# Two cross attentions: projections, splitting and stacks two slots sooner, the maxima's transfers ahead of the stacks'

## The reference, cut to what matters

```python
x = x + g_msa * (attn(rope(q), rope(k), v, mask) @ attn_out_W)   # self attention, 128 keys
x = x + g_x * (attn(xc @ cq_W, ctx @ ck_W, ctx @ cv_W) @ co_W)   # first cross attention, 77 keys
x = x + g_mlp * (gelu(xm @ mlp_W1 + b1) @ mlp_W2 + b2)
x = x + (attn(xq @ Wq + bq, xkv @ Wkv + bkv) @ Wp + bp)          # second cross attention, 77 keys
```

## Time and profile before

| | |
|---|---|
| median of three executions | 1186.53 us (1183.35 to 1187.0) |
| the profiled execution | 1197.59 us, span 1195.8 us |
| busy share of the span | PE 90%, ACT 71%, POOL 72%, DVE 69%, PEld 52% |
| granted TensorE clock, mean | 0.946 of full |
| self attention's units | from 81.2 us (L812 of unit 0) |
| first cross attention's units | 428.5 to 718 us |
| second cross attention's units | from 908.9 us |

### The profile page before, as it was taken

How to read it: one execution, slowest core, us unless ns; L and a number is a source line. 1 busy time by engine, 2 the same in 40 slices (tenths; PEclk the granted TensorE clock), 3 DMA queues, 4 the chain that set the end, 5 groups by cost and what they waited for, 6 DMA issues and landing times.

```text
span 1195.8 us, 42336 instructions
## 1 busy us (share of the span) xinstructions
PE 1080.7 (90%) x16226; PEld 616.5 (52%) x16226; DVE 825.0 (69%) x2195; ACT 851.5 (71%) x1527; POOL 856.6 (72%) x1804
## 2 busy tenths in 40 slices
PE   5779999999998889888998888999998999999987
PEld 4435555555544445554554553444444566666665
DVE  4358888888887878777887662322325888878775
ACT  2347776777766688787887667787875878878765
POOL 2578888888886678677887424676887878888742
PEclk9789999999998999898999679999998999999988
DMA  6766567665664566666766610000315677777761
GB/s 164 182 129 109 103 111 136 107 108 101 110 111 78 77 102 94 100 102 100 106 99 105 97 20 1 1 0 1 57 20 73 113 119 124 124 119 127 117 111 33
DMA packets 165018, 110.40 MB, mean 92 GB/s; under 512 B 42553, under 2 KB 164434, under 8 KB 164818
## 3 DMA queue, kind: packets, MB, share of 16 engines
q1 hardware_dynamic: 161744, 105.97, 52.8%
q10 hardware_dynamic: 3074, 1.72, 0.6%
HBM read 9.71 MB, written 4.19 MB: 12 GB/s over the span
## 4 chain that ended last, share of the span: by engine, by line
PE 54%; ACT 11%; POOL 8%; SPq 7%; DMA 6%; DVE 5%; issue 5%; ACTq 1%; POOLq 0%; DVEq 0%
PE ps_po L535 10%; PE ps_pj L433 7%; SPq L1004 6%; PE ps_st L514 6%; DMA stacks<-mt 6%; PE ps_nat L486 5%; ACT p L812 5%; PE ps_pj L416 5%; PE ps_pj L411 4%; PE ps_st L547 4%; PE ps_po L556 4%; PE ps_nat L471 3%; PE ps_pj L424 3%; DVE negmax L619 2%; ACT nrm L781 2%
## 5 line engine op out<-in xcount | busy, mean ns | idle before, releaser
L619 DVE TENSOR_REDUCE negmax<-ps_nat 128x8 f32<-128x616 f32 (+1 forms) x384 | 360.6, 939 | 62.3 <-PE ps_nat L486 51.9
L812 ACT ACTIVATE p<-ps_st 128x1024 f32<-128x1024 f32 (+1 forms) x256 | 261.3, 1021 | 165.2 <-PE ps_st L514 164.2
L535 PE MATMUL ps_po<-p,vz 77*32 77x128 f32 (+1 forms) x6144 | 262.0, 291 | 4.7 <-DVE mt L627 2.2
L514 PE MATMUL ps_st<-stacks 64*77 64x128 bf16 (+1 forms) x3072 | 161.0, 227 | 39.2 <-DMA stacks<-mt 28.9
L812 ACT ACTIVATE p<-ps_st,key_bias 77x1024 f32<-77x1024 f32 x128 | 142.1, 1110 | 62.0 <-PE ps_st L514 60.9
L535 PEld LDWEIGHTS ps_po<-p,vz 77*32 77x32 f32 (+1 forms) x6144 | 153.4, 113 | 46.3 <-issue 13.5
L896 POOL TENSOR_TENSOR ot<-vv,den 128x128 f32<-128x128 f32 x192 | 87.7, 457 | 122.7 <-ACT den L800 111.6
L486 PEld LDWEIGHTS ps_nat<-stacks 64*128 64x128 bf16 x3072 | 79.7, 98 | 138.8 <-issue 125.4
L486 PE MATMUL ps_nat<-stacks 64*128 64x77 bf16 (+1 forms) x3072 | 136.4, 211 | 10.4 <-DVE negmax L619 7.2
L514 PEld LDWEIGHTS ps_st<-stacks 64*77 64x77 bf16 (+1 forms) x3072 | 109.9, 113 | 53.4 <-issue 26.9
L627 DVE COPY mt<-ps_po 128x128 bf16<-128x128 bf16 x192 | 42.5, 221 | 112.5 <-PE ps_po L500 112.2
(11 more groups left out here) (149 smaller groups left out, 2112.0 us busy)
## 6 DMA issues: line engine op xcount, KB each, us to landing
stacks<-parts SPq DMA_DIRECT2D x512, 128.0 KB, 3.3
stacks<-parts SPq DMA_DIRECT2D x256, 77.0 KB, 2.8
stacks<-mt SPq DMA_DIRECT2D x192, 32.0 KB, 2.8
p<-in_x_dram SPq DMA_DIRECT2D x16, 256.0 KB
out_dram<-part SPq DMA_DIRECT2D x16, 256.0 KB, 2.3
ot<-in_ctx_dram SPq DMA_DIRECT2D x8, 154.0 KB
gated<-in_ctx_dram SPq DMA_DIRECT2D x8, 154.0 KB
stacks<-in_L_xcond_adaLN_W_dram SPq DMA_DIRECT2D x1, 576.0 KB, 4.3
```

The source lines that it names most:

```text
L514: m = t.matmul(c.ps_st[h][0:nk, S * g:S * g + S], kst[half(h), par, at, nk * j:nk * j + nk], qst[half(h), par, at, S * j:S * j + S], start ...
L535: m = t.matmul(c.ps_po[step % 2][32 * g:32 * g + 32, S * p:S * p + S], c.vz[0:nk, i % 2, step % G, g, at:at + 32], c.p[0:nk, hh, S * g:S * ...
L619: v.tensor_reduce(c.negmax[:, step % 2, :].rearrange("p (h q g) -> p h q g", h=2, q=2)[:, :, p, :], c.nat_pair[:].rearrange("p (h n) -> p ...
L812: a.activation(c.p[0:nk, 2 * p:2 * p + 2, :].rearrange("p h n -> p (h n)"), c.st_pair[0:nk, :], ACT.Exp, bias=bias).then_inc(exped, 1)
```

## The change

1. `head_of(i)`: in both cross attentions b becomes u - 22. With it q, k, the norm's three jobs (centring 13 slots ahead of b for all groups that are not placed early), the splitting on ACT and POOL and the stack transfers all come two slots sooner. For groups 16 to 19 the norm comes three slots sooner, since it was 12 ahead of b. Group 35's norm moves from slots 289 and 290 to 281 and 282, as early jobs in the MLP.
2. `v` moves from u-2 to u-4 in the cross attentions. `o` moves from u+16 to u+15 for groups 14 to 31, and in the second cross attention `o` from u+16 to u+14 and `o2` from u+17 to u+15. DVE's reading of the first cross attention's o thereby goes from an odd slot to an even one. The last group's o stays.
3. SP: `bring_max` stands ahead of the slot's stack transfers, in all attentions. In the cross attentions the 16 stack transfers are spread over seven slots in place of six, two in each slot that has a maximum: modulo 8, 1 (two), 2 (three), 3 (two), 4 (three), 5 (two), 6 (three), 7 (one).
4. `key_slots` is b+8 instead of b+7: an even slot.

Modulo 8 the first cross attention has afterwards on PE: m 0, q 1, k 3, v 4, c 5, o 7.

```diff
+def head_of(i):
+    return slot_of(PER * i) - LEAD - (2 if i >= NG else 0)
...
-            b = slot_of(PER * i) - LEAD
+            b, u = head_of(i), slot_of(PER * i)
...
-            if 2 * NG <= i < 2 * NG + 4:
-                self.norm_early(("n", i), b - 6)
+            if i < NG:
+                self.norm(("n", i), b - 6, 3 if i >= 1 else 0)
+            elif 2 * NG <= i < 2 * NG + 4:
+                self.norm_early(("n", i), b - (6 if i < 2 * NG + 3 else 12))
             else:
-                self.norm(("n", i), b - (6 if i < NG else 12 if i < NG + 4 else 13), 3 if 1 <= i < NG else 0)
-            self.add(self.late, b + (14 if i < NG else 18), ("v", i))
-            if i < 2 * NG:
-                self.add(self.late, b + LEAD + (17 if i < NG - 2 else 16), ("o", i))
-                self.add(self.late, b + LEAD + (17 if i < NG - 2 else 16), ("o2", i))
-            else:
-                self.add(self.late, b + LEAD + (12 if i == GROUPS - 1 else 16), ("o", i))
-                self.add(self.late, b + LEAD + (12 if i == GROUPS - 1 else 17), ("o2", i))
+                self.norm(("n", i), b - 13)
+            self.add(self.late, u - (6 if i < NG else 4), ("v", i))
+            first, second = (u + 12, u + 12) if i == GROUPS - 1 else (u + 14, u + 15) if i >= 2 * NG else (u + 15, u + 15) if i >= NG - 2 else (u + 17, u + 17)
+            self.add(self.late, first, ("o", i))
+            self.add(self.late, second, ("o2", i))
...
-            key_slots = {slot_of(PER * i) - LEAD + 7: i for i in range(NG, 2 * NG)}
+            key_slots = {head_of(i) + 8: i for i in range(NG, 2 * NG)}
...
-                      1: ((7, 0, (0, 1, 2)), (8, 0, (3,)), (8, 1, (0, 1)), (9, 1, (2, 3)), (9, 0, (4,)), (10, 0, (5, 6, 7)), (11, 1, (4, 5, 6)), (12, 1, (7,)))}
+                      1: ((7, 0, (0, 1)), (8, 0, (2, 3, 4)), (9, 1, (0, 1)), (10, 1, (2, 3)), (10, 0, (5,)), (11, 0, (6, 7)), (12, 1, (4, 5, 6)), (13, 1, (7,)))}
...
+                if even(unit_at(slot + 3)):
+                    bring_max(unit_at(slot + 3) // 2)
                 for i, x, t in at_slot.get(slot, []):
                     bring_stack(i, x, t)
-                if even(unit_at(slot + 3)):
-                    bring_max(unit_at(slot + 3) // 2)
```

More of the change, by code:

```diff
@@ L827, in _ @@
                 for r, x, which in steps[min(i // NG, 1)]:
-                    at_slot.setdefault(slot_of(PER * i) - LEAD + r, []).append((which, i, x))
+                    at_slot.setdefault(head_of(i) + r, []).append((which, i, x))
             a.preload_act_table_set("natural_log_exp_and_others")
@@ L1015, in _ @@
                 for r, x, ts in starts[min(i // NG, 1)]:
-                    at_slot.setdefault(slot_of(PER * i) - LEAD + r, []).extend((i, x, t) for t in ts)
+                    at_slot.setdefault(head_of(i) + r, []).extend((i, x, t) for t in ts)
             def fetch(i):
```

## The result

The changed kernel takes 1150.24 us, the median of four executions (1149.43 to 1151.61); the kernel before, timed beside it, takes 1185.3 (1183.35 to 1187.0, four). The ratio is 0.9677, with an interval of 0.9639 to 0.9715: 35 us faster. The prediction was 1162, with a range of 1147 to 1182. The profiled execution of the changed kernel took 1151.61 us with a span of 1149.8; its mean granted clock is 0.968.

The account below looks back on a forecast made before the run. The prediction took PE's stands for late maxima transfers, and half clock behind them, as what could be won. Terms 15.2 + 5.1 + 2.5 + 2 + 4 + 0 + 0 = 28.8 us, 25 carried to the median: 1186.5 - 25 = 1162 us, range 1147 to 1182.

Parts of the forecast that it names:

- What bounds the kernel: Cross attentions: a group takes 16.6 us when nothing is late; PE's avoidable wait is for the maxima's transfer, 28.9 us.
- SP's queue: Cross attentions: bunching starts maxima's transfers late, PE stands beyond 2.4 us lateness; ordering and spreading make these waits nearly vanish.
- at 16.9 each: Eleven groups in each cross attention were to take 16.9 us each, gaining 15.2 us in the first, 5.1 in the second.
- The cost of one transfer: SP's queue: 0.72 us for one transfer, halfway between 0.64 and 0.80; 20 transfers take 14.4 of a group's 16.6 us.
- From the profiled execution to the median: Whole kernel: 25 of the 28.8 us gained against the profiled 1197.6 us carried over to the median of 1186.5.
- The rule on landing: DMA queues: if landing counts rather than starting, order wins nothing and the time stays at 1186.5 us.
- Group 35's norm: Second cross attention's start: moving this norm into the MLP removes PE's 3.86 us wait for POOL; gain 4 us.
- The self attention's end: Norms of groups 16 to 19: new waits against old ones removed, 0; bounds a gain of 4 and loss of 6 us.
- The hidden edits: Cross attentions: jobs turn by two slots together, only o's reading changes its relation; taken as 0, bounds -3 and +5 us.
- Half of it: Rival: stands go, but the clock still falls or groups take 17.4 us; about 1174 us, chance 0.17.
- no change: Rival: landing or ACT is what counts, time stays within 0.3%, at 1186 us; chance 0.08.
- The banks: Slower rival, first cross attention: q takes o's bank, so a late DVE makes PE wait; 1203 us, chance 0.13 for slower.

Follow-up runs that it names:

- run 8: The kernel before with the maxima's transfers issued by ACT, behind its exponential, instead of SP; nothing else moved: 1158.28 us, ratio 0.9706.
- 5: The changed kernel with the old, bunched list of stack transfer starts, the maxima still first: 1163.4 us, ratio 0.9783.
- run 6: The changed kernel with the maxima behind the slot's stack transfers, the spread starts kept: 1171.02 us, ratio 0.9853.
- run 2: The changed kernel with both SP edits undone (old list of starts, maxima last), the other edits kept: 1203.06 us, ratio 1.013.
- run 7: The kernel before with only group 35's norm moved, to slots 283 and 284 instead of 289 and 290: 1188.27 us, ratio 0.999.
- run 4: The changed kernel with the norms of groups 16 to 19 three slots later, where they stood before: 1153.14 us, ratio 0.9663.
- run 11: The changed kernel with the norms of groups 16 to 19 one slot later: 1157.22 us, ratio 0.973.
- run 10: The changed kernel with only the key row moved back to b+7, an odd slot: 1149.02 us, ratio 0.9666.
- 12: The changed kernel itself, unaltered, timed once more: 1151.45 us, ratio 0.9677.
- run 1: The kernel before with one edit, the maxima's transfer ahead of the slot's stack transfers: 1173.65 us, ratio 0.9854.
- run 3: The changed kernel with o of groups 14 to 31 one slot sooner, so DVE reads it in an odd slot: 1175.05 us, ratio 0.9839.
- run 9: The changed kernel with o of groups 14 to 31 and the key row each one slot sooner: 1158.99 us, ratio 0.9745.

## Why the prediction was right, step by step

**What bounds the kernel: right.** The waits for the maxima were the one thing that could go, and a group without them takes what the earlier trace rows showed for the quick one, or less.

**SP's queue: the mechanism was right, its worth was mis-sized.** The chain of the argument (bunching makes the maxima start late, PE stands, the clock drops to its lower level) held at its first links: run 8 for the start, the waits of runs 5 and 6 for both of the two edits, run 2 for nothing else doing it. The last link, from the stand to half clock, holds for the longer stands and not for each (last section). Mis-sized was the term "at 16.9 each": the groups take 16.3 and 16.4. I had taken 16.6 as the floor because no group of before was quicker, and added 0.3 for groups that would not reach it. The floor was a little lower, and all but one of them reached it in the first attention, all but two in the second. That is 5.8 and 5.5 us too little in the two attentions; in the group behind the first eleven it is 3.5 more, and the rest of that attention with the MLP brings 3.5 that I had not counted at all, though its clock of 0.94 stood open to it. Its first 47 us still run at a clock of 0.85 (0.75 before), without a wait for a transfer; PE's longest stand in them is 1.13 us for POOL's splitting. Why the clock falls there is open.

**The cost of one transfer.** I took 0.72 us, between 0.64 and 0.80. The lateness of 1.63 us in slot 7 lies between what 0.72 gives (0.5) and 0.80 (1.95): from slot 1 to slot 7 of a 16.3 us group 12.2 us pass, and (12.2 + 1.6) / 18 = 0.77 us for a transfer. In the stretch shown above it is less, 18 transfers from 562.72 to 575.62, 0.72 each. The tolerance of 2.4 us held, so the figure cost the changed kernel nothing, but it is why run 6 missed.

**From the profiled execution to the median.** I carried 25 of 28.8 us over, since that execution lay 11 us above the median. The profiled executions differ by 46.0 and the medians by 35: the caution was right and too small, 4 us where 11 was due. So the forecast is 12 us too high by two errors that partly cancel: the terms of the sum are 17 us too small, and the step to the median took off 7 us too little. The measured 1150 lies inside the range, 3 us above its lower end, and that the forecast came this near owes something to this cancelling.

**The rule on landing** that I had set against the change (the Trainium skill, "DMA: Bandwidth & Descriptors", section "Issuing engines are not separate DMA queues") says that the time to start a DMA is usually small relative to the DMA. If that decided here, the time would have stayed at 1186.5. Landing stayed at 2.7 to 2.8 us and the time fell by 35 us; run 8 alone gives 2.9% by moving the issue to another engine (1158.3 us beside 1191.8). Here the measurement decides: each start is short against its landing, but 20 of them at 0.72 to 0.77 us take 14 to 15 of a group's 16.3 us, and so their order counts.

**Group 35's norm** was counted at 4 and gave 3.7 in the profile. Run 7 warns against reading it as a gain by itself.

**The self attention's end** was counted at 0 and came out at +1.5, inside the bound of 6. The wait that I named (POOL for the values of group 14) is there with 3.18 us. The old placing is no better by the total (run 4) and one slot later is worse (run 11). A small cost is likely all the same: the five groups take 116.6 to 118.9 us in the four profiles with these lists (the changed kernel, 5, 10 and 12), 113.4 to 115.1 in the four with the heads and norms of before (1, 7, 8 and the kernel before), and 115.6 in run 4.

**The hidden edits** were taken at 0. For the edits as made that holds; the key row in the other slot changes nothing (run 10). But I wrote that the place of `o` is the one relation that changes, and overlooked the key row, which edit 4 moves by one slot and not by two, into the norm's. And my reason, that DVE is not last in a slot, is refuted by run 3: with `o` one slot sooner the copy of the maxima is late behind a DVE instruction that has tripled, and each group costs 1.2 us more. I had looked at the sums of work per slot and not at what runs beside what.

**The rivals.** Half of it and no change did not come. The banks did not make PE wait: in the changed kernel it waits once for a reading of `o` (L420 for L663), 0.8 us, and that behind the first cross attention's units.

**The signs I had named.** The wait for `mt` is under 5 us, and the 3.86 us wait at the second's start is gone. The groups take 16.2 to 16.3 us, just under the 16.4 to 17.0 named. "Within 1 us of its copy's end" is met in slots 1, 3 and 5 and missed in slot 7, with 1.63 us at the median.

## What to carry to other kernels

Where an engine waits for a transfer, take the time from the producer's end to the start of the issue, and compare it with the lateness at which the first waits appear; a queue that is fast enough on the average can still be late by its own bunching. Putting one transfer first moves the lateness to those behind it, so ordering and spreading belong together, and another engine's queue is a third way that here cost nothing. When jobs turn by a slot, check which short VectorE instruction comes to stand beside which GpSimd instruction and which of them starts first, not only the sums of work in a slot.

## What the runs showed of the hardware

DVE's multiplication of 128x308 uint8 into bf16, both in SBUF, takes 0.43 us, and 1.33 us when it starts just behind POOL's f32 multiplication of 1.27 us; it then ends 0.18 us behind it. That is as if DVE stood until POOL was done. The Trainium skill, "SBUF — State Buffer", section "Who interferes with whom", says that a VectorE instruction in a mode that uses two ports, which `tensor_scalar` can enter, contends with GpSimd: the first of the two to issue gets the port pair that both share for its whole instruction, and the other blocks. In which mode this instruction ran no trace shows; the two ends, at 577.47 and 577.65 us, agree with the rest. DVE's reading of PSUM right behind it (L614) takes 0.68 us there as in the changed kernel, with POOL's next operation beside it.

Who pays depends on who starts first. In the changed kernel the key row comes first, and it is POOL's multiplication that grows, from 1.27 to 1.36 to 1.41 us:

```profile
565.57 0.43 DVE L704 TENSOR_SCALAR parts<-gated,key_factor 128x308 bf16<-128x308 uint8 x1
565.75 1.38 POOL L938 TENSOR_TENSOR ht<-xc,nrm 128x512 f32<-128x512 f32 x1
```

So 0.3 us of difference between two starts turn a cost of 0.1 us into one of 0.9. Started 0.56 us behind the norm, the key row takes 0.89. The border isn't exact in the rows: once, in run 6, the key row's row starts 0.09 us ahead of the norm's, and it takes 1.53 us all the same.

A DMA that ACT issues beside its own activation took 0.54 us and lengthened none that shows: nine groups of ACT's work are 133.4 us busy in run 8 and 133.3 in run 9, where SP issues it.

Long stands of PE come with half clock in these traces, short ones only at times. In the kernel before, the four stands of 1.67 to 2.62 us for a transfer of the maxima have the clock at half within about 1 us of their end. Of those of 1.0 to 1.5 us some have and some haven't; behind one of 1.48 us that ends at 987.10 the clock stays up. In run 1 it is so for the stack transfers, too: down behind 1.83 and 1.84 us, up behind 1.43. And the clock also falls with no such stand: in the changed kernel it is at half from 623.4 to 626.8 us, while no wait of PE from 447 to 627 us is longer than 0.6 us. The first line is of the kernel before, the second of the changed one:

```profile
987.10:997.10 10.00, 9.84 (x179) 6.05 (x181) 7.07 (x21) 8.59 (x15) 7.58 (x19) 1.00 0.78 129
623.40:626.80 3.40, 3.40 (x32) 1.51 (x32) 1.91 (x7) 1.76 (x3) 3.17 (x9) 0.50 0.87 147
```
